# The second gate of a graph kernel in another order: left tiles one pair ahead, the sums at the head of a round, three of its left tiles multiplied on GpSimd

## What is computed

```python
hg = jnp.einsum('bnf,gf->bng', h3, Wg[:, :F])          # nodes: 8 graphs x 8 nodes
qg = jnp.einsum('blf,gf->blg', q, Wg[:, F:]) + bg      # queries: 8 graphs x 64
attn = jax.nn.sigmoid(hg[:, :, None, :] + qg[:, None, :, :])
qi = jnp.einsum('bnlf,blf->bnf', attn, q)              # sum over the 64 queries
alpha = jax.nn.sigmoid(h3 @ Wq[:, :F].T + qi @ Wq[:, F:].T + bq)
hn = alpha * jnp.tanh(qi) + (1.0 - alpha) * h3
```

## Time and profile before

| | |
|---|---|
| median of 3 runs | 280.14 us (279.99 to 280.22) |
| profiled execution, device time | 279.79 us |
| its span in the profile | 278.0 us |
| PE busy | 257.1 us (92%) |
| DVE busy | 149.3 us (54%) |
| ACT busy | 94.3 us (34%) |
| POOL busy | 93.9 us (34%) |

### The profile page before, as it was taken

One profiled execution on the slowest core, in us unless ns is written; L12 is line 12 of the kernel. 1 busy time (PEld: TensorE's weight loads), 2 busy tenths in 40 slices (PEclk: granted clock), 3 DMA queues, 4 the chain that ended last, 5 costly groups with the idle time before them and its releaser, 6 DMA issues.

```text
span 278.0 us, 4579 instructions
## 1 busy us (share of the span) xinstructions
PE 257.1 (92%) x1889; PEld 134.0 (48%) x1889; DVE 149.3 (54%) x264; ACT 94.3 (34%) x159; POOL 93.9 (34%) x80
## 2 busy tenths in 40 slices
PE   8899999999899989899996789899999988998994
PEld 4566854455345532477761223235564443433572
DVE  1844630019999999630058797975622236114423
ACT  2312520035759976120025656761311022003000
POOL 7670000003999999000026789870000000000000
PEclk9999999999999999999999999999999999999999
DMA  7999996992008937005999800000699063000001
GB/s 244 374 401 402 400 397 191 409 402 105 1 0 288 387 112 241 0 2 177 407 402 400 317 0 2 0 2 0 208 405 400 11 225 118 0 0 2 0 2 28
DMA packets 21062, 51.87 MB, mean 187 GB/s; under 512 B 4137, under 2 KB 4393, under 8 KB 21042
## 3 DMA queue, kind: packets, MB, share of 16 engines
q1 hardware_dynamic: 20352, 51.25, 49.6%
q10 hardware_dynamic: 690, 0.34, 0.5%
HBM read 51.39 MB, written 0.20 MB: 186 GB/s over the span
## 4 chain that ended last, share of the span: by engine, by line
PE 61%; DVE 13%; POOL 10%; issue 7%; ACT 3%; DMA 3%; SPq 1%; DVEq 0%; POOLq 0%; ACTq 0%
PE ps L1012 12%; PE ps L980 10%; POOL prod L550 10%; PE ps L1128 6%; PE ps L1358 6%; PE ps L1027 4%; PE ps L954 4%; DVE pre L846 4%; DMA W<-in_L_gnn_Wg 3%; DVE prod L832 3%; PE ps L1097 3%; PE ps L1244 2%; PE ps L1187 2%; PE ps L1218 2%; ACT pre L626 2%
## 5 line engine op out<-in xcount | busy, mean ns | idle before, releaser
L550 POOL TENSOR_TENSOR prod<-pre,qn 128x768 f32<-128x768 f32 x38 | 73.9, 1965 | 11.1 <-ACT pre L626 9.5
L846 DVE TENSOR_TENSOR pre<-ps,qg 128x768 f32<-128x768 f32 x49 | 45.5, 949 | 6.6 <-PE ps L1218 5.8
L626 ACT ACTIVATE pre<-pre 128x768 f32<-128x768 f32 x49 | 41.3, 847 | 17.9 <-DVE pre L846 17.1
L1218 PE MATMUL ps<-stack,bsel 96*128 96x384 bf16 x128 | 31.5, 329 | 5.5 <-DVE pre L846 3.2
L1128 PE MATMUL ps<-W 128*128 128x384 f32 x96 | 34.4, 489 | 0.2 <-ACT W L412 0.2
L412 ACT COPY W<-ps 128x384 f32<-128x384 f32 x41 | 18.4, 483 | 38.7 <-PE ps L954 38.5
L1244 PE MATMUL ps<-prod,rsel 128*32 128x384 f32 x256 | 27.3, 497 | 3.1 <-POOL prod L550 2.4
L540 POOL COPY stack<-hi 32x384 bf16<-32x384 bf16 x4 | 2.2, 553 | 76.8 <-DVE hi L802 76.7
L1218 PEld LDWEIGHTS ps<-stack,bsel 96*128 96x128 bf16 x128 | 9.0, 97 | 33.1 <-DVE pre L846 16.0
L1128 PEld LDWEIGHTS ps<-W 128*128 128x128 f32 x96 | 17.4, 190 | 9.9 <-issue 0.9
L1012 PE MATMUL ps<-W,prod 128*64 128x256 f32 (+1 forms) x240 | 20.6, 328 | 0.0
(11 more groups left out here) (190 smaller groups left out, 277.5 us busy)
## 6 DMA issues: line engine op xcount, KB each, us to landing
W<-in_L_gnn_W SPq DMA_DIRECT2D x9, 2304.0 KB, 11.5
W<-in_L_gnn_W_rel SPq DMA_DIRECT2D x6, 2304.0 KB, 15.4
W<-in_L_gnn_W_root SPq DMA_DIRECT2D x2, 2304.0 KB, 9.9
W<-in_L_gnn_Wq SPq DMA_DIRECT2D x4, 1152.0 KB, 8.0
W<-in_L_gnn_Wg SPq DMA_DIRECT2D x3, 1152.0 KB, 13.3
qn<-in_L_gnn_query_embs SPq DMA_DIRECT2D x4, 384.0 KB, 10.2
W<-in_L_gnn_Wg SPq DMA_DIRECT2D x3, 384.0 KB, 3.9
xa<-in_x ACTq DMA_DIRECT2D x2, 96.0 KB, 6.3
```

Of the source, the lines that this page charges most:

```text
L550: nc.gpsimd.tensor_tensor(prod[:, T % PRODS, :], pre_of(T), qn[:, pair_and_node(t)[0], :], ALU.mult).then_inc(prod_p, 1)
L626: nc.scalar.activation(dst, src, ACT.Sigmoid).then_inc(sig_ready, 1)
L846: nc.vector.tensor_tensor(dst, ring(T), by_half(qg[:, pair_and_node(t)[0], :]), ALU.add).then_inc(pre_ready, 1)
L1218: ins = nc.tensor.matmul(ring(T)[:, c, :], bsel[:, t // 2, :], stack[:, c, t % 2, :], start=KINDS[T] not in TENSOR_ADD, stop=True)
```

## The change

In the second gate only, the following is new; the first gate issues what it did.

- The kinds become "DP DP XP DP PP DP XP DP PP DP XP DP PP DP XX DD". TensorE puts `qg` under 10 tiles instead of 5, VectorE adds it to 22 instead of 26. GpSimd multiplies 17 tiles instead of 18: the right tiles of pairs 0 to 13, and the left tiles of pairs 4, 8 and 12. VectorE multiplies 15 instead of 14.
- `copy_queries` has four multiplications of 64 rows by 64 output rows instead of two of 128 by 128. For this each half of `qg` must also lie on the other 64 partitions: `qs`, which two DMA transfers from `qg` fill. They stand in SyncE's queue where the load of `L2_W1_1` stood, and use its slot; that load now waits until the last sum of the gate.
- The node rows no longer go through `stack`. `add_nodes_rows` multiplies `hi`, `mid` and `low` in place, with 32 rows each: 12 multiplications for two tiles, instead of four with 96 rows. GpSimd makes two thirds of `low` and VectorE one third; the copies into `stack` and the four pieces of line 818 are gone.
- Ring: left tiles take two slots in turn, right tiles always the third. The products have eight buffers instead of four (`more_prod`).
- A round k of TensorE's loop has, in this order: the sum of pair k-3, `qg` under left tile k+1 where its kind is D, and then the nodes of left tile k+1 and right tile k together. VectorE's round: product of left tile k, product of right tile k-1, addition to left tile k+1, addition to right tile k (each where the kind asks for it).
- The other 128 columns of `alpha` leave the loop's end: two of six chunks now stand behind the last sum, four behind the transposes, and two `keep_warm` there are gone.

The core of the diff:

```diff
-            "TD" "PX" "PX" "PP" "PD" "PX" "PX" "PP" "PX" "PD" "PX" "PP" "PX" "PD" "PX" "XD")
+            "DP" "DP" "XP" "DP" "PP" "DP" "XP" "DP" "PP" "DP" "XP" "DP" "PP" "DP" "XX" "DD")
@@ SyncE
-            load("L2_W1_1", a["L2_gnn_W1"][1], rgcn_done, done + 3)
+            sp.wait_ge(rgcn_done, done + 3)
+            for c in range(2):
+                sp.dma_start(qs[c * N:(c + 1) * N, :, :],
+                             qg[(1 - c) * N:(2 - c) * N, :, c * HD:(c + 1) * HD]).then_inc(qs_loaded, 16)
             load("L2_W1_2", a["L2_gnn_W1"][2], rgcn_done, done + 4)
             load("L2_W2_0", a["L2_gnn_W2"][0], hg_done, 2)
+            load("L2_W1_1", a["L2_gnn_W1"][1], reduced, TILES)
@@ GpSimd
+                if layer == 1:
+                    pool.wait_ge(mid_part, 1)
+                    nc.gpsimd.tensor_tensor(low[:, 0:CUT], t1[:, 0:CUT], mid[:, 0:CUT], ALU.subtract).then_inc(low_ready, 1)
@@ VectorE, second gate
+                    add(right(0))
+                    multiply(left(0))
+                    for k in range(1, HALF_T):
+                        multiply(left(k))
+                        multiply(right(k - 1))
+                        if k + 1 < HALF_T:
+                            if KINDS[left(k + 1)] in "XP":
+                                add(left(k + 1))
+                            add(right(k))
+                    multiply(right(HALF_T - 1))
@@ TensorE
+            def copy_queries(T):
+                p = pair_and_node(T % TILES)[0]
+                for c in range(2):
+                    rows = slice(c * N, (c + 1) * N)
+                    nc.tensor.matmul(ring(T)[rows, c, :], ident[rows, rows], qg[rows, p, c * HD:(c + 1) * HD],
+                                     start=True, stop=False)
+                for c in range(2):
+                    rows = slice(c * N, (c + 1) * N)
+                    other = slice((1 - c) * N, (2 - c) * N)
+                    nc.tensor.matmul(ring(T)[other, c, :], ident[rows, rows], qs[rows, p, :], start=True, stop=False)
+            def add_nodes_rows(tiles):
+                for part in (hi, mid, low):
+                    for T in tiles:
+                        t = T % TILES
+                        for c in range(2):
+                            rows = slice(c * N + t % 2 * GN, c * N + (t % 2 + 1) * GN)
+                            ins = nc.tensor.matmul(ring(T)[:, c, :], bsel[rows, t // 2, :], part[rows, :],
+                                                   start=(part is hi and KINDS[T] != "D"), stop=(part is low))
+                        if part is low:
+                            ins.then_inc(hg_cast, 1)
+            def second_gate():
+                add_nodes_rows((left(0), right(0)))
+                add_nodes_rows((left(1),))
+                add_bias_alpha(1, 0)
+                project_alpha(1, 0, nodeT, WqT_h, range(2))
+                for k in range(1, HALF_T):
+                    if k >= LAG:
+                        reduce_pair(left(k - LAG), k == LAG, False)
+                    if KINDS[left(k - 1)] == "P":
+                        wait_added(pe, left(k - 1))
+                    else:
+                        wait_multiplied(pe, left(k - 1))
+                    if k + 1 < HALF_T:
+                        if KINDS[left(k + 1)] == "D":
+                            copy_queries(left(k + 1))
+                        wait_added(pe, right(k - 1))
+                        add_nodes_rows((left(k + 1), right(k)))
+                    else:
+                        copy_queries(right(k))
+                        add_nodes_rows((right(k),))
+                    if k < LAG:
+                        keep_warm(2, ACC)
+                    if k in ALPHA_AT:
+                        project_alpha(1, 0, nodeT, WqT_h, [ALPHA_AT[k]])
+                for k in range(HALF_T - LAG, HALF_T):
+                    reduce_pair(left(k), False, k == HALF_T - 1)
+                add_bias_alpha(1, 1)
+                project_alpha(1, 1, nodeT, WqT_h, range(2))
```

More of the change, by code:

```diff
@@ L145, in ring_slot @@
             t = T % TILES
[L146 to L151, removed]
+            if T < TILES:
+                return t % 2
+            return t // 2 % 2 if t % 2 == 0 else 0 if t == TILES - 1 else 2
         def ring(T):
@@ L338, in alpha_bank @@
         def alpha_bank(layer, part):
[L339 removed]
+            return TRB if part == 0 else (5, 2)[layer]
         def alpha_psum(layer, part):
             return ps[:, alpha_bank(layer, part), 0:CUT if part == 0 else HD - CUT]
[L344 removed]
+        ALPHA_AT = {TILES - KC + k: k for k in range(KC)}
         def late_groups(t):
@@ L819, in stack_low @@
                                             ALU.subtract).then_inc(lo_stacked[g], 1)
-                for g in range(2):
-                    for h in range(2):
-                        stack_low(g, h)
+                if layer == 0:
+                    for g in range(2):
+                        for h in range(2):
+                            stack_low(g, h)
+                else:
+                    nc.vector.tensor_tensor(low[:, CUT:HD], t1[:, CUT:HD], mid[:, CUT:HD], ALU.subtract).then_inc(low_ready, 1)
                 LAG = 2
@@ new lines, in add @@
+                def add(T):
+                    wait_cast(dve, T)
+                    if KINDS[T] != "X":
+                        wait_pre_free(dve, T)
+                    dst = ring(T) if KINDS[T] == "X" else by_half(pre_of(T))
+                    nc.vector.tensor_tensor(dst, ring(T), by_half(qg[:, pair_and_node(T % TILES)[0], :]),
+                                            ALU.add).then_inc(pre_ready, 1)
+                if layer == 0:
+                    for t in range(TILES + LAG):
+                        if t % (TILES // 2) == 0 and t < TILES:
+                            wait_units_out(dve, UNITS // 2 * (1 + t // (TILES // 2)))
+                        if t < TILES:
+                            add(t)
+                        if t >= LAG:
+                            multiply(t - LAG)
+                else:
[9 more added lines that the diff above has]
+                    multiply(right(HALF_T - 1))
@@ new lines, in reduce_pair @@
+            def reduce_pair(T, first, last):
+                k = T % TILES // 2
+                s = GN - 1 - k // NB * 2 * NB - k % NB
+                for g in range(2):
+                    wait_multiplied(pe, T + g)
+                for c in range(2):
+                    for g in range(2):
+                        at = c * N + g * GN
+                        ins = nc.tensor.matmul(ps[at:at + GN, ACC, 0:HD], rsel[:, s:s + GN],
+                                               prod_of(T + g)[:, c * HD:(c + 1) * HD],
+                                               start=first, stop=last, skip_group_check=True)
+                ins.then_inc(reduced, 1)
```

195 lines of the change are left out of this document (95 added, 100 removed).

## The result

| | before | changed kernel |
|---|---|---|
| median | 280.18 us (279.99 to 280.29) | 283.47 us (282.13 to 284.17, 4 runs) |
| profiled execution | 279.79 us, span 278.0 | 283.86 us, span 282.1 |

The ratio is 1.0101, 95% interval 1.0072 to 1.013: the change makes the kernel slower by 1%. 277.6 was forecast, with 281.0 as the upper end of the range and 0.16 for slower.

A forecast was written before the change was run, and what follows sets the result against it. VectorE was taken to set the pace, a loop of latencies where pairs have fewer operations. Gate gain 3.36 less 0.79 given back took 279.79 to 277.2; the median's 0.35 made 277.6 us, range 276.2 to 281.0.

The forecast's parts named there:

- the head: Start of second gate: `qs` lands 2.5 us after 142.5, at 145.0; first nodes start at 146.46, 0.2 earlier than before.
- My upper bound, 4.0 by pieces: Transfer time of `qs` at the gate's start if 512 half-length pieces each cost as much as one of 768: 4.0 us.
- first nodes to round 1: Start of the gate's rounds: streaming and drain, hand-overs, VectorE's addition and first product take 2.6 us.
- round 1 to the end of the last sum: Rest of the gate's rounds: 18.3 with left additions, 13.1 without plus waits, then 3.5 and 3.4 us at the end.
- Nodes for two tiles: TensorE's node multiplications in each round: 12 bfloat16 instructions, four at a time, stream 0.50 us, 0.67 with drain.
- Rivals 1: Nodes: weight loads of four row groups go one after another, nodes take 1.17 us, kernel slower at 285.3; chance 0.13.
- 2: Nodes: the next wave's loads wait for the wave in flight, nodes take 0.78 us, total 279.6; chance 0.09.
- `qg` under a tile: TensorE's copy of `qg` under a D tile: 8 float32 instructions on four array quarters take 0.65 us, before 1.3.
- Rival 3: Copy of `qg`: it runs two quarters at a time, 1.3 more at the head, total 280.1, no difference; chance 0.09.
- GpSimd's loop: Rounds: GpSimd, not VectorE, ends last once in four rounds, its three products delaying a sum; 9.70 us per four rounds.
- Given back behind it: Behind the last sum: bias, `alpha` chunks and transposes take 2.12 us instead of 1.33 before; 0.79 lost.
- At nothing: One select more on GpSimd at the start and the later load of `L2_W1_1` cost no time.

The follow-up runs named there:

- experiment 1: Changed kernel with the two `qs` transfers issued ahead of the load of `L2_W1_0` instead of behind it; 276.88 us, ratio 0.9861.
- experiment 9: Changed kernel with the load of `L2_W1_2`, behind `qs` in SyncE's queue, held until `qs` has landed; 280.94 us, ratio 1.0012.
- experiment 2: Changed kernel with 22 `keep_warm` multiplications in TensorE's wait for `qs`; 281.69 us, ratio 1.0037.
- experiment 8: Changed kernel without `qs` and its transfers, `qg` under all ten D tiles by old full-size multiplications; 279.14 us, ratio 0.9942.
- experiment 5: Changed kernel with `qs` ahead of the load of `L2_W1_0` and left tiles of pairs 4, 8, 12 of kind X; 273.76 us, ratio 0.9756.
- Experiment 6: Kernel of experiment 5 with bias and two `alpha` chunks ahead of the last sum instead of behind it; 274.16 us, ratio 0.9767.
- Experiment 3: Changed kernel with `qg` under the first two tiles in the old full-size form, `qs` waited for only in round 2; 278.02 us, ratio 0.9906.
- experiments 7: Changed kernel with the two `qs` transfers issued by ScalarE in a queue of its own; 282.80 us, ratio 1.0077.
- 4 (the same transfers): Changed kernel with left tiles of pairs 4, 8 and 12 of kind X instead of P, multiplied by VectorE; 279.85 us, ratio 0.9967.

## Why the prediction was wrong

**The step that failed is the head: "I take 2.5, nearer to the bytes, so 145.0".** `qs` was there at 148.9. My upper bound, 4.0 by pieces, was the right price for the pieces: in experiment 1 they flow from 136.8 to 140.6, and 512 pieces of 120 ns on 16 engines are 3.8. From 142.5 that makes 146.5. The rest I had no term for, since I took the queue as in order: the load behind `qs` runs among its last pieces and costs 2.2 (experiment 9). 146.5 + 2.2 = 148.7, beside the measured 148.9.

That this sum comes out is partly luck, for the queue was not what it says. The pieces did not wait for the load ahead to land: they began at 140.7, and by 145, with or without a load behind them, 486 of the 512 were through, while the load ahead landed only at 145.5. What TensorE waited for are the last 26, until 147.1 with nothing behind them (146.7 without the later start of that execution) and 148.9 with the next load. Why these 26 lag is not shown.

**The second part of the failure stood in no rival: what TensorE's clock does in the wait.** The forecast itself had a wait of 1.3 us there, and I priced none but the waiting. Idle from 144.06 to 148.92, TensorE came back at 0.50 and stayed there to 154: 2.3 us in the profiles (experiment 2).

In the profiled executions the forecast and the measurement differ by 6.65 us (a span 2.57 shorter against one 4.08 longer). The account:

| step | forecast | changed kernel | later by | experiment 1 |
|---|---|---|---|---|
| `qg` starts | 145.06 | 148.92 | 3.86 | 144.28 |
| to the first nodes | 1.40 | 2.77 | 1.37 | 1.47 |
| first nodes to round 1 | 2.6 | 3.67 | 1.07 | 2.62 |
| round 1 to the end of the last sum | 38.3 | 38.73 | 0.4 | 38.76 |
| to the multiplication with the sums | 2.12 | 2.03 | -0.09 | 2.03 |

The first three rows are 6.3 of it, and experiment 1 gives all three back and 0.7 more.

The other steps held, one by one:

- *Nodes for two tiles*, forecast 0.67 with drain: measured 0.67. Rivals 1 and 2 are out. The cited rule of the Trainium skill (page "TensorE: Matmul & The Clock Gate", Part 3) on weight loads and its 3.07 times are not what this trace shows: the waves follow at 0.16, as single instructions did.
- *`qg` under a tile*, 0.65, four quarters together: L1247 and L1252 start within 0.02 and the eight end after 0.86 with drain (161.82 to 162.19 + 0.49). Rival 3 is out. The old form costs 1.3 at the head and, over the gate, 42.73 - 41.38 = 1.35 (experiment 8).
- *GpSimd's loop*, 9.70 per four rounds: 9.80 and 9.78. The sum behind a P left tile waits for it, as said, by 1.30. This was a cost of the change that I had counted and not questioned: without the P tiles the gate is 2.8 shorter (experiment 5).
- *Given back behind it*, 2.12: 2.03. Experiment 6 shows that the chunks stand well where they are.
- *At nothing*: GpSimd's part of `low` lasts 0.67, and `low` is ready at 145.31, before `qs`. One select more at the start makes GpSimd 0.35 longer there (four in 1.25 us, three in 0.90 before), and TensorE has no wait for it. The late load of `L2_W1_1` is never waited for; behind 196.12 both spans have the same length.
- Experiment 3 is the forecast with the late `qs` taken out, and its 278.02 stands beside 277.6.

So the mechanism in the rounds was right in its terms, and the change lost at its head more than it gained behind it.

## What to carry to other kernels

When a change puts a small on-chip transfer in front of the engine that bounds the kernel, count it in pieces as well as in bytes, since the last piece decides; add what is queued ahead of it and what runs beside its end; and issue it ahead of the bulk loads, which alone was worth 6.6 us here (283.47 - 276.88). Price a wait of TensorE with the clock that comes back behind it, 2.3 us here. And once the order has changed, look again at which engine has which work: three left products on GpSimd cost 2.8 us in the new one.

## What was not expected of the hardware

- Pieces of 1536 bytes within the chip's buffers took 121 ns of a DMA engine, those of 3072 bytes from main memory 120: the rate fell from 400 to 218 GB/s with the engines full.
- A transfer is not finished in order with its queue: the last 26 pieces of `qs` came while the load behind already ran, at 319 to 390 GB/s in all.
- TensorE's clock fell to 0.50 in an idle time of 4.86 us and also in experiment 9, behind one of 2.67; with `keep_warm` in the wait it did not fall.
- The landing of `qs` differed from profile to profile: TensorE's wait for it was 4.9, 4.3 and 3.8 us in those of the changed kernel and of experiments 7 (another queue) and 4 (the same transfers). The spread of the times cannot be put down to it, though: the changed kernel's four lie 2.0 us apart and those of experiment 9 3.3, but those of the kernel before, which has no `qs`, lie up to 2.4 apart where it was timed beside the experiments.
- Why the load ahead of `qs` lands 3.0 us later than before (14.2 us to landing, 13.6 in experiment 9) is only partly settled: pieces of both were under way from 140.7 on, and from 141 to 144 only 16 packets were longer ones, beside 428 of under 2 KB. How the engines share them was not tried.
